# Gate projections of three feed-forward stages: one wide matmul for the high and low weight parts, and an addition on VectorE in place of ScalarE's copies

## The reference

```python
x = x + tanh(g_xattn[l]) * xattn_l(layernorm(x), ctx_4096, ...)
x = x + tanh(g_ffn[l])   * ffn_l(layernorm(x), ...)
```

```python
gate_probs = softmax(xf @ gate_W.T)
weights, sel = top_k(gate_probs, 2)          # renormalised to sum 1
w_dense = zeros((T, 8)).at[rows, sel].add(weights)
h = einsum('td,erd->ter', xf, A) * (w_dense[:, :, None] * 2.0)
out = xf @ W_base.T + einsum('ter,eor->to', h, B)
```

## Time and profile before

| what | value |
|---|---|
| median of 3 runs | 1760.56 us (1758.3 to 1760.56) |
| the profiled execution | 1759.71 us, of which 1757.9 us are the span in the trace |
| mean granted TensorE clock | 0.998 of full speed |
| busy | PE 98%, PEld 81%, DVE 69%, POOL 55%, ACT 49% |
| instructions | 27515 in all, 8776 matmuls |

### The profile page before, as it was taken

How to read it: one execution, slowest core, us unless ns; L and a number is a source line. 1 busy time by engine, 2 the same in 40 slices (tenths; PEclk the granted TensorE clock), 3 DMA queues, 4 the chain that set the end, 5 groups by cost and what they waited for, 6 DMA issues and landing times.

```text
span 1757.9 us, 27515 instructions
## 1 busy us (share of the span) xinstructions
PE 1731.3 (98%) x8776; PEld 1429.6 (81%) x8776; DVE 1210.2 (69%) x2202; ACT 863.4 (49%) x2459; POOL 972.8 (55%) x808
## 2 busy tenths in 40 slices
PE   7999999999999999999999999999999999999999
PEld 6888887776878888888888888888888888888887
DVE  7566666878876666666666677766666666666685
ACT  7666665735444454444444454344444454444451
POOL 3223232556584666657566564666574666756561
PEclk9999999999999999999999999999999999999999
DMA  6101010020110111101111011011110101101101
GB/s 212 30 15 37 13 34 7 22 104 30 43 43 19 54 30 36 42 18 48 30 42 38 28 35 49 18 55 35 31 42 18 54 30 36 42 18 51 33 13 49
DMA packets 37429, 69.47 MB, mean 40 GB/s; under 512 B 4426, under 2 KB 5194, under 8 KB 37234
## 3 DMA queue, kind: packets, MB, share of 16 engines
q1 hardware_dynamic: 37362, 68.61, 13.0%
HBM read 66.50 MB, written 2.10 MB: 39 GB/s over the span
## 4 chain that ended last, share of the span: by engine, by line
PE 93%; DVE 3%; issue 1%; POOL 1%; ACT 1%; DMA 0%; SPq 0%; POOLq 0%; DVEq 0%
PE ps L443 28%; PE ps L445 27%; PE ps L444 27%; PE ps L715 4%; PE ps L696 3%; PE ps L622 1%; PE ps L653 1%; DVE negmax L1598 1%; DVE ot_lo L1631 0%; DVE pt_loL L1620 0%; POOL rope_a L3424 0%; DMA ct_raw<-in_ctx_t 0%; DVE ot_lo L1626 0%; PE ps L1080 0%; PE ps L1081 0%
## 5 line engine op out<-in xcount | busy, mean ns | idle before, releaser
L3442 POOL TENSOR_TENSOR probs<-probs,rsums 128x512 f32<-128x512 f32 (+1 forms) x160 | 194.5, 1215 | 274.5 <-DVE rsums L1616 274.5
L3424 POOL TENSOR_TENSOR rope_a<-rope_a,rope_b 128x512 f32<-128x512 f32 x160 | 206.7, 1292 | 155.1 <-DVE rope_b L1591 154.9
L443 PE MATMUL ps<-wo_hiL,ot_hi 128*128 128x512 f32 x608 | 245.7, 404 | 2.9 <-DVE ot_lo L1631 2.0
L443 PE MATMUL ps<-xt_hi,wq_hiL 128*128 128x512 f32 x608 | 243.4, 400 | 0.3
L445 PE MATMUL ps<-wo_hiL,ot_lo 128*128 128x512 f32 x608 | 238.5, 392 | 0.0
L444 PE MATMUL ps<-wo_loL,ot_hi 128*128 128x512 f32 x608 | 237.8, 391 | 0.0
L445 PE MATMUL ps<-xt_hi,wq_loL 128*128 128x512 f32 x608 | 237.7, 391 | 0.0
L444 PE MATMUL ps<-xt_lo,wq_hiL 128*128 128x512 f32 x608 | 236.9, 390 | 0.0
L2643 ACT ACTIVATE probs<-ps,negmax 128x128 f32<-128x128 f32 x512 | 182.0, 373 | 90.3 <-DVE negmax L1598 90.2
L2660 ACT CAST ot_hi<-ps 128x512 fp32r<-128x512 f32 (+1 forms) x160 | 90.8, 568 | 251.3 <-PE ps L445 251.3
L3436 POOL TENSOR_TENSOR q_loL<-rope_a,q_hiL 128x512 fp32r<-128x512 f32 x128 | 164.6, 1297 | 29.7 <-ACT q_hiL L2630 29.7
(11 more groups left out here) (232 smaller groups left out, 4260.9 us busy)
## 6 DMA issues: line engine op xcount, KB each, us to landing
raw<-in_L_proj SPq DMA_DIRECT2D x108, 256.0 KB, 2.6
raw<-in_L_out SPq DMA_DIRECT2D x76, 256.0 KB, 2.6
raw<-in_F_w SPq DMA_DIRECT2D x16, 256.0 KB, 2.8
ct_raw<-in_ctx_t SPq DMA_DIRECT2D x8, 256.0 KB, 6.4
x<-in_x SPq DMA_DIRECT2D x8, 256.0 KB, 6.4
cn_raw<-in_ctx SPq DMA_DIRECT2D x8, 256.0 KB, 7.4
out<-x SPq DMA_DIRECT2D x8, 256.0 KB, 2.0
raw<-in_L_kv SPq DMA_DIRECT2D x6, 256.0 KB, 3.0
```

Of the source, the lines that this page charges most:

```text
L443: pe.matmul(dst, l_hi, r_hi, start=start, stop=False)
L3424: gp.tensor_tensor(rope_a[:, a], rope_a[:, a], rope_b[:], ALU.add).then_inc(L.s_rsum, 1)
L3442: gp.tensor_tensor(pv, pv, rsums[:, b % 2].unsqueeze(2).to_broadcast([P, GH, L.keys]), ALU.mult).then_inc(L.s_p, 1)
```

## The change: what it does

- The two weight buffers `ag_hi` and `ag_lo` of a stage become one, `ag_two` (high part first, the same bytes at the same place).
- `gates` runs, for each chunk, one matmul of the tokens' high part against both weight parts at once, into a PSUM region of twice the columns (144, 272 or 276), and one of the tokens' low part against the high weights, into the first half of it. That is 8 matmuls per batch instead of 12; the columns streamed are the same, 12 times the stage's columns.
- The second half of the region is a partial sum that has to be added. ACT's `taken` copies it, in one piece, into a new buffer `gx` (which shares its place with `st`), and signals a new semaphore `f_rest`. A new step on DVE, `summed`, adds the first half (from PSUM) and `gx`, in two pieces, into `probs` and `gl`, and signals `f_ev`. So PE's wait for batch b - 2, and `logits`, now hang on DVE.
- The lists `bridge`, `middle` and `end` are written anew on PE, DVE, ACT and POOL: the same steps plus 24 times `summed`, in another order. The loops of A2 and A3 and the lists of the first three groups of A0 stay.

```diff
-        st = new("st", [P, GH * P], F32)
+        r_st = region(GH * P * 4)
+        st = at("st", [P, GH * P], F32, r_st)
+        gx = at("gx", [P, 2, P + NE + 2], F32, r_st)
...
-                ag_hi=at(f"ag_hi{f}", [P, C, n], F32R, at_a) if er else None,
-                ag_lo=at(f"ag_lo{f}", [P, C, n], F32R, at_a + 2208) if er else None,
+                ag_two=at(f"ag_two{f}", [P, 2, C, n], F32R, at_a) if er else None,
...
+                both = ps[:, 2 + b % 2, 0:2 * F["cols"]].rearrange("p (s n) -> p s n", s=2)
                 for c in range(C):
-                    mm = triple(pe, ps[:, 2 + b % 2, 0:F["cols"]], xt_hi[:, c, rows], xt_lo[:, c, rows],
-                                F["ag_hi"][:, c], F["ag_lo"][:, c], c == 0, c == C - 1)
+                    if c < C - 1:
+                        pe.matmul(both, xt_hi[:, c, rows], F["ag_two"][:, :, c], start=c == 0, stop=False)
+                    pe.matmul(both[:, 0], xt_lo[:, c, rows], F["ag_two"][:, 0, c], start=False, stop=False)
+                mm = pe.matmul(both, xt_hi[:, C - 1, rows], F["ag_two"][:, :, C - 1], start=False, stop=True)
                 mm.then_inc(f_h, 1)
...
+            def summed(f, b):
+                er, cols = FF[f]["er"], FF[f]["cols"]
+                v.wait_ge(f_rest, FM[f] + b + 1)
+                v.tensor_tensor(probs[:, b * P:b * P + er], ps[:, 2 + b % 2, 0:er], gx[:, b % 2, 0:er], ALU.add)
+                v.tensor_tensor(gl[:, b, 0:cols - er], ps[:, 2 + b % 2, er:cols], gx[:, b % 2, er:cols],
+                                ALU.add).then_inc(f_ev, 1)
...
                 act.wait_ge(f_h, FM[f] + b + 1)
-                act.copy(probs[:, b * P:b * P + er], ps[:, 2 + b % 2, 0:er])
-                act.copy(gl[:, b, 0:cols - er], ps[:, 2 + b % 2, er:cols]).then_inc(f_ev, 1)
+                if FM[f] + b >= 2:
+                    act.wait_ge(f_ev, FM[f] + b - 1)
+                act.copy(gx[:, b % 2, 0:cols], ps[:, 2 + b % 2, cols:2 * cols]).then_inc(f_rest, 1)
```

Of the lists, the parts that the prediction speaks of. PE's list in `end` (F3), from the last output projection of A3:

```diff
                 a3.out_proj(7, last)
                 products(3, 0)
+                gates(3, 4)
+                norm_transpose("F3", 5)
                 norm_transpose("F3", 6)
                 products(3, 1)
-                gates(3, 4)
+                products(3, 2)
+                norm_transpose("F3", 7)
+                turn(3, 0)
                 gates(3, 5)
-                turn(3, 0)
-                norm_transpose("F3", 7)
                 gates(3, 6)
                 experts(3, 0)
                 experts(3, 1)
                 gates(3, 7)
```

DVE's list in `end`, same place:

```diff
                 a3.residual(7, last)
                 a3.next_stats(7, last)
                 logits(3, 0)
+                norm_rows("F3", 6)
+                threshold_gate(3, 0)
                 norm_tail("F3", 5)
-                threshold_gate(3, 0)
                 norm_tail("F3", 6)
                 norm_rows("F3", 7)
                 weigh(3, 0)
+                summed(3, 4)
                 turned(3, 0)
```

More of the change, by code:

```diff
@@ L1161, in middle @@
                 products(2, 1)
+                gates(2, 5)
                 turn(2, 0)
@@ L1243, in end @@
                 norm_transpose("F3", 0)
+                a3.transposes(5, last)
                 a3.scores(7, last)
-                norm_transpose("F3", 1)
                 a3.out_proj(4, last)
@@ L1254, in end @@
                 gates(3, 1)
+                a3.out_proj(6, last)
                 norm_transpose("F3", 3)
-                a3.out_proj(6, last)
+                a3.heads_out(7, last)
                 norm_transpose("F3", 4)
-                a3.heads_out(7, last)
                 gates(3, 2)
-                norm_transpose("F3", 5)
                 gates(3, 3)
@@ L1298, in bridge @@
                 a0.transposes(1, last)
-                a0.fillers(2, last, only=0)
                 a0.out_proj(0, last)
                 a0.heads_out(1, last)
-                a0.fillers(2, last, only=1)
+                a0.scores(3, last)
                 a0.transposes(2, last)
-                a0.scores(3, last)
+                a0.fillers(2, last, only=0)
                 a0.out_proj(1, last)
                 a0.heads_out(2, last)
+                a0.fillers(2, last, only=1)
                 a0.scores(4, last)
                 a0.transposes(3, last)
+                a0.out_proj(2, last)
+                a0.heads_out(3, last)
+                a0.scores(5, last)
                 pe.wait_ge(Lq[0].s_qk, Lq[0].ready("KQ", last, 1))
@@ L1311, in bridge @@
                 norm_transpose("F0", 0)
-                a0.out_proj(2, last)
-                a0.heads_out(3, last)
-                norm_transpose("F0", 1)
-                a0.scores(5, last)
                 a0.transposes(4, last)
@@ L1414, in bridge @@
                 products(1, 7)
+                a2.begin(5, 0)
                 a2.begin(3, 1)
@@ L2076, in middle @@
-                norm_rows("F2", 3)
                 a2.pt_tail(6, last)
                 a2.row_sum(7, last)
+                a2.next_stats(3, last)
                 norm_tail("F2", 1)
+                norm_rows("F2", 3)
                 a2.residual(5, last)
                 a2.next_stats(4, last)
+                summed(2, 0)
+                norm_tail("F2", 2)
                 a2.ot_tail(6, last)
+                norm_tail("F2", 3)
+                a2.pt_tail(7, last)
+                summed(2, 1)
@@ L2093, in middle @@
+                summed(2, 3)
+                logits(2, 0)
+                a2.residual(7, last)
+                top2_gate(2, 0, 0)
                 norm_tail("F2", 5)
-                logits(2, 0)
-                norm_rows("F2", 6)
-                top2_gate(2, 0, 0)
                 top2_gate(2, 0, 1)
-                a2.residual(7, last)
+                summed(2, 4)
                 top2_gate(2, 0, 2)
+                norm_tail("F2", 6)
                 top2_gate(2, 0, 3)
-                norm_tail("F2", 6)
@@ L2140, in middle @@
                 a3.begin(3, 1)
+                a3.begin(5, 0)
+                residual(2, 7)
                 norm_shift("A3", 5)
-                residual(2, 7)
+                norm_shift("A3", 6)
                 next_stats("A3", f_x, 7, FN[2])
-                norm_shift("A3", 6)
                 a3.begin(4, 0)
@@ L2219, in end @@
                 norm_rows("F3", 4)
                 a3.next_stats(5, last)
+                a3.residual(6, last)
+                summed(3, 0)
                 norm_tail("F3", 3)
-                a3.pt_tail(7, last)
-                a3.residual(6, last)
+                summed(3, 1)
+                a3.ot_tail(7, last)
                 norm_rows("F3", 5)
+                summed(3, 2)
+                a3.next_stats(6, last)
+                summed(3, 3)
                 norm_tail("F3", 4)
-                a3.ot_tail(7, last)
@@ L2286, in bridge @@
                 a0.pt_tail(4, last)
-                a0.residual(3, last)
+                norm_rows("F0", 1)
                 norm_rows("F0", 2)
                 a0.row_sum(5, last)
-                norm_tail("F0", 0)
+                a0.residual(3, last)
                 a0.next_stats(3, last)
@@ L2334, in bridge @@
                 logits(0, 1)
+                next_stats("A1", f_x, 1)
+                residual(0, 2)
+                norm_shift("A1", 0)
+                norm_shift("A1", 1)
                 top2_gate(0, 1, 0)
@@ L3031, in middle @@
                 a2.pt_head(5, last)
-                a2.exps(6, last)
+                a2.exps(7, last)
                 a2.o_head(5, last)
                 a2.pt_head(6, last)
-                norm_head("F2", 1)
-                a2.exps(7, last)
+                a2.base_weight(3)
+                norm_head("F2", 2)
+                expert_weight(2)
+                a3.weights(0)
+                taken(2, 0)
                 a2.o_head(6, last)
+                norm_head("F2", 3)
+                taken(2, 1)
```

892 lines of the change are left out of this document (446 added, 446 removed).

## The result

| | median of the runs | runs | ratio to the kernel before |
|---|---|---|---|
| before | 1759.86 us | 4, 1758.3 to 1760.56 | |
| after | 1748.03 us | 4, 1746.31 to 1749.82 | 0.9936, 95% interval 0.9924 to 0.9948 |

11.8 us less. The forecast of 1749.3 us is 1.3 us above the median, and the time is well inside the range of 1745 to 1755.5. The profiled execution took 1746.31 us, with a span of 1744.5: 13.4 us less than that of the kernel before, of which 11.0 were forecast.

The account below looks back on a forecast made before the run. PE was taken to bound the kernel, busy 1731.3 of 1757.9 us. Matmuls 10.1 + hw wait 0.7 + clock 1.7 - new waits 1.5 = 11.0 us less, 1748.7 or 1749.6 by baseline; predicted 1749.3 us, range 1745 to 1755.5.

Parts of the forecast that it names:

- The wide matmul: Gate blocks on PE in F0, F2, F3: 8 matmuls instead of 12 save 3.6, 3.3 and 3.2 us, together 10.1.
- nothing changes: Rival, chance 0.05: the 272-column matmul costs 0.2275 us, only F0 gains 3.6 us, waits cost 1.5; 1758 us.
- columns alone set the time: Rival, chance 0.02: columns stay as many, so PE gains nothing from the matmuls; 1759 us.
- the 0.7 us for `hw`: F3: PE's wait for DVE's hw goes, 0.7 us less.
- VectorE's sums: DVE in F0, F2, F3: additions take 10.7 us more, bounds 9.0 and 15.3, hidden in DVE's idle time.
- ScalarE: ACT's gate copies: two of 268 and 173 ns become one of some 0.27 us; 4 us off ACT, worth 0.
- The margins: PE's steps that wait for DVE in F0, F2, F3: counted room 0.5 to 2 us, only 0.1 at out_proj(7).
- New waits of 1.5 us in A1, F1 and A2: Stretches behind F0 where DVE is busiest: 1.5 us taken for all new waits, bounds nothing and 6.8.
- The first rival: VectorE takes the gain back in part, 6.8 us of waits instead of 1.5; 1754.6 us, chance 0.15.
- A0's rewritten list: A0's last group, 2.0 us wait for ot_lo: bounds 2 us gained and 2 lost, taken as 0.
- The clock: F0: the fall to 1.2 GHz after three gate blocks in a row goes, 1.7 us less, bounds 0 and 1.7.
- The slower rival: Gates wait for DVE's sums; sums 0.8 us late cost over 3.5 us, 1.2 us late give 1770; chance 0.05.

Follow-up runs that it names:

- e2: The changed kernel with each wide matmul issued as two of half the columns, sums and new lists kept: 1758.71 us, ratio 0.9996 to the kernel before.
- e3: The changed kernel without DVE's sums, the second half of each gate result left out: 1748.01 us, ratio 0.9935 to the kernel before.
- e4: The changed kernel with each pair of sums done twice, first into a spare buffer: 1748.65 us, ratio 0.9935 to the kernel before.
- e5: The kernel before with PE's gates(0, 4) moved behind out_proj(7), so no three gate blocks run in a row there: 1762.39 us, ratio 1.0027.
- e6: The kernel before with the wide matmul and the sums put by hand into DVE's old list, nothing else moved: 1762.6 us, ratio 1.0024.
- e9: Wide matmul and sums in the old lists, with four of the sums moved in DVE's list: 1756.54 us, ratio 0.9982 to the kernel before.
- e1: The changed kernel's new lists with the old gate projection of 12 matmuls, two ACT copies and no sums: 1759.32 us, ratio 1.0003.
- e8: The changed kernel with ot_tail(5) put ahead of row_max(7) in DVE's list of A0's last group: 1746.64 us, ratio 0.9932.
- e10: The changed kernel measured a second time, nothing altered: 1747.86 us, ratio 0.9930 to the kernel before.
- e11: Second measurement of the changed kernel with ot_tail(5) ahead of row_max(7) in DVE's list: 1746.89 us, ratio 0.9927.
- e7: The changed kernel with PE's gates(0, 4) ahead of norm_transpose(5) and out_proj(7), three gate blocks in a row: 1751.25 us, ratio 0.9956.
- e12: The changed kernel without DVE's sums and with PE's gates(0, 4) ahead of norm_transpose(5) and out_proj(7): 1751.38 us, ratio 0.9947.

## Why the prediction was right, point by point

- **The wide matmul** was the gain, as forecast: 9.2 us measured for 10.1, and e2, which takes back the merging alone, loses all of it. The term is 0.9 us too large, spread evenly: over its eight blocks a stage saved 3.3 us in F0 for 3.6, 2.95 in F2 for 3.3 and 2.9 in F3 for 3.2. The rivals in which nothing changes and in which columns alone set the time are refuted: the columns are as many as before. The price of the first of them, 1758, left out the 0.7 us for `hw` and the 1.7 of clock that the second one counts; with them it would have been 1755 to 1756. By the isolated gap that the Trainium skill gives ("TensorE: Matmul & The Clock Gate", section "Back-to-back issue gap") a block's time goes with its columns, and e2 and the changed kernel should have been alike; they differ by 2.9 us in F2. The same section says that this formula under-counts where narrow matmuls and weight loads alternate, and with that the trace agrees: 0.115 us at 136 columns, where the formula gives 59 ns.
- **VectorE's sums** cost 9.9 us of instructions for 10.7 forecast, and nothing of the time, as forecast (e3, e4). That the busy time would rise by about 10 was wrong: it rose by 4.7, of which the sums are 6.3 (1214.9 against e3's 1208.6), and the rest of DVE's list is 1.6 us shorter.
- **ScalarE**: one copy of 273 ns in place of two, worth nothing, as forecast.
- **The margins.** In F3 `turn(3, 0)` was given 0.4 us of room. It has none. DVE's `weigh` and GpSimd's operations beside it, then the transposes that read it, in the changed kernel:

```profile
1716.08 1.99 DVE L1961 TENSOR_TENSOR hw<-probs,gt 128x128 f32<-128x128 f32 x4
```

```profile
1711.74 1.29 POOL L3430 TENSOR_TENSOR lb_lo<-raw,lb_hi 128x512 fp32r<-128x512 f32 x1
1716.25 1.47 POOL L3607 TENSOR_TENSOR x<-x,bias 128x512 f32<-128x512 f32 x1 [3.22 <-DVE xn L1517]
```

```profile
1718.13 0.66 PE L1001 MATMUL ps<-consts,hw 128*128 128x128 f32 x4
```

  `weigh` ends at 1718.07, and `turn` starts 0.06 us later, the same distance as in the kernel before, e5, e6 and e9, where PE was idle for it. It starts 0.21 us behind the transpose ahead of it, where such a transpose takes 0.11 (and in e1 and e2, where `weigh` is done in time, `turn` follows after 0.11). So it waits by about 0.1 us, too short for the list of waits.

  What the forecast had of this place is wrong in two parts that nearly cancel. `weigh` begins 8.3 us after the residual (1707.75) and not 6.1; 1.7 of the 2.2 us more are in the threshold chain, which takes 4.0 us for 2.3. And `weigh` takes 1.99 us for 3.06. At its old duration PE would have waited for a microsecond more, so the step came out right by luck.

  Both durations go with where GpSimd's work falls. In the trace before, two of `weigh`'s four multiplications take 1.37 and 1.36 us, beside these two operations of GpSimd:

```profile
1725.66 1.46 POOL L3570 TENSOR_TENSOR x<-x,bias 128x512 f32<-128x512 f32 x1 [3.75 <-DVE xn L1512]
1727.08 1.33 POOL L3393 TENSOR_TENSOR lb_lo<-raw,lb_hi 128x512 fp32r<-128x512 f32 x1
```

  After, one takes 1.38 and the others 0.28, and `lb_lo` now runs at 1711.74 beside the threshold chain, where two operations take 0.79 and 1.23 us that took 0.17 and 0.19 before. It is the order and not chance: `weigh` in F3 takes 3.04 to 3.06 us in all four profiles with the old lists and 1.99 to 2.01 in all ten with the new ones. No experiment moved GpSimd's work alone.
- **New waits of 1.5 us in A1, F1 and A2** did not come; waits of all feed-forward stretches fell a little. The first rival, VectorE taking part of the gain back, had this for its price, and is refuted.
- **A0's rewritten list**, put at 0 with 2 us either way, costs 1.1 us of waits: 0.3 in front of `out_proj(6)`, where a wait of 1.78 us has become one of 2.07, and 0.8 in waits of 0.2 to 0.4 us from 315 on, as the 0.36 for `pt_loL` at 347.58.
- **The clock.** The fall in F0 is gone, as forecast, for 1.7 us. A second fall in the trace before, from 421 to 425 in A1, is gone too, 1.4 us. The prediction read the clock in the stages of the change alone, and this lies behind them. Busy time and clock before:

```profile
421.00:425.00 4.00, 4.00 (x13) 2.94 (x12) 3.93 (x8) 2.98 (x5) 3.49 (x3) 0.59 0.17 37
```

  The reason I gave, three narrow blocks in a row, is not what it takes: e1 and e2 have F0's blocks by two and still a fall, at 389 to 390, and a mean granted clock below 1.000 in every one of their 20 runs. Between `gates(0, 0)` and the last matmul, the profiles of the kernels with 12-matmul gates and no new wait (before, e1, e2) show one or two falls; the six with the wide matmul and no new wait (the changed kernel, e3, e4, e8, e10, e11) show none; the four with wide matmuls and a new wait among F0's gates (e6, e7, e9, e12) at least one. That goes with the change, but e4 and e12 have a fall at 308, too, in a part of A0 that is the same in all of them and where the other twelve profiles have none. So a fall is not a matter of the kernel's instructions alone.

  What the change brings beyond the one profile can be read from the mean granted clock that is on record for every run, since a fall of 3.4 us at half the rate takes 0.001 off it: the profile before, with two falls, has 0.998, those of e1 and e2, with one, 0.999, the one after 1.000. The kernel before has 0.999 in 34 and 0.998 in 23 of the 57 runs that stand beside the experiments, and in none 1.000; their mean times are 1758.6 and 1760.6 us, one fall apart. The changed kernel has 1.000 in eight of its nine runs (e10's among them) and 0.999 in one. So one or two falls went in nearly every execution. An estimate from these counts is 1.4 falls before and 0.1 after, at 1.7 us each: 2.2 us on average, where the two profiles happen to show 3.1. The medians agree: e1 and e2 are 10.7 to 11.3 us above the changed kernel against 9.2 for the matmuls, which leaves 1.5 to 2.1. With one fall less the kernel before would take about 1756.7 us, and the eight runs of the changed one at 1.000 average 1747.5: about 9.2 us for all else, as much as the gate blocks alone. Among the kernels without new waits the falls go with the unmerged matmuls and not with the old order, as e1 and e2 have the new one; why is open.
- **The slower rival** had the right mechanism and the right point to decide it: it is e6. What kept it away is the new order, which I had gone through but counted at nothing in the sum.

The errors of the sum, against the two profiles, have opposite signs: 0.9 too much on the matmuls and 1.1 on A0's waits, 1.8 too little on new waits, 1.4 on the clock and 0.9 on the start of the span.

## What to carry to other kernels

Where PE issues narrow matmuls at a fixed distance, as here in float32r with a weight load for each, two that share the stationary operand are worth merging, even if the halves must be added elsewhere: count matmuls, not columns, up to the 276 columns tried. But shortened blocks leave less time for the copy and the sum that their successors wait for, so most of such a gain was only had with a new order: in the old one all of it, and 0.2% on top, went into late sums, falls of the clock at them and the rest of the order, and moving four sums gave back a part (e9). Where the trace names one releaser of a wait, look at what else that engine finishes in the microsecond before, since the second one may be nearly as late. And when a step of one engine moves, look at what it now runs beside on the others: here `weigh` got shorter and the threshold chain longer by more than the margin that had been counted.

## What the runs showed of the chip

- Matmuls of 72 and 144 columns in turn start 0.22 us apart in pairs, those of 136 and 272 columns 0.24. The split is uneven: 0.15 and 0.075 us in F0, 0.18 and 0.06 in F2. A wide one's surplus is made up by the narrow one behind it.
- A fall of the clock to 1.2 GHz lasts 3.4 us and takes 1.7; one, in e9, lasts 6.8. Of the twelve between PE's first and last matmul in the 14 profiles, six come within 2 us of the end of a wait of 0.77 to 3.2 us among narrow matmuls or transposes (three in e6, one each in e7, e9 and e12), four of them after it and two (e9's and the last of e6) while PE is still idle. It is no rule: the falls at 370.55 in the kernel before and at 390 and 389 in e1 and e2 have no wait of 0.15 us or more in the 10 us ahead, and waits of 1.38 us (e9, F3), 1.35 us (e5) and 2.07 us (the changed kernel, A0) had no fall behind them. Nor is it the same each time. In A0 all profiles have a wait of about 1 us for `probs` at 306; in e4 and e12 the clock falls behind it, in the others not. Busy time and clock of e4:

```profile
308.00:312.00 4.00, 3.52 (x16) 3.02 (x15) 3.31 (x5) 1.46 (x3) 3.34 (x3) 0.58 0.21 58
```

- The same multiplication of two SBUF operands of 128 columns on DVE (one of the four of `weigh`) takes 0.28 us or 1.34 to 1.40. In the 14 profiles every one of the 18 long ones ran beside an operation of GpSimd; others did so too and stayed at 0.28, so what makes the difference is open.
